# VectorE's order in a fused attention and feed-forward kernel: one maximum ahead of the shares, and the finish of y ahead of the masking

## What is computed

```python
x = x + conv_ref(ln_over_channels(x))       # clustering attention
t = tokens(x)
t = t + ffn_ref(layernorm(t))               # feed-forward, 96 -> 384 -> 96
return images(t)

# conv_ref, for each head and each quarter image (28 x 28 tokens)
centers = pooled(f)                         # 4 x 4 centers
sim = sigmoid(beta + alpha * cosine(centers, tokens))
sim = sim * one_hot(argmax over centers)    # "masked"
agg = (sim @ v + vc) / (sim.sum + 1)        # "reciprocal", "shares"
out = sim.T @ agg, then the projection Wp and its bias

# ffn_ref
h = quantize(norm(t) @ sign(W1) + b1)       # scale: largest |h| of a group of 6 images
y = quantize(gelu(h) @ sign(W2) + b2)       # scale: largest |y| of the group
# quantize(a) = clip(a * 128 / (largest + 1e-5), +-(128 - 1e-5))
```

## Time and profile before

| | us |
|---|---|
| median of 3 runs | 3051.05 |
| lowest and highest | 3048.34, 3052.36 |
| the profiled execution's own time | 3054.72 |
| its span in the trace | 3052.90 |

### The profile page before, as it was taken

The page is one execution under the profiler, slowest core; times in us unless marked ns, Lnnn a source line. Parts: engine busy times, 40 slices in busy tenths (PEclk is TensorE's granted clock), DMA queues, the critical chain, the costliest instruction groups (busy, mean ns, idle before and its releaser), DMA issues.

```text
span 3052.9 us, 62593 instructions
## 1 busy us (share of the span) xinstructions
PE 2839.2 (93%) x20918; PEld 1957.2 (64%) x20918; DVE 2680.4 (88%) x5540; ACT 2172.5 (71%) x4510; POOL 1869.5 (61%) x4275
## 2 busy tenths in 40 slices
PE   3999999999999999999999999999999999999984
PEld 2666676556666765666666666666655766666553
DVE  3788888899999989899998999999989999998954
ACT  2677777887777779767776977677788777677941
POOL 1566666347777753677776357777734777774353
PEclk9999999999999999999999999999999999999976
DMA  1011111002222210222221012222100222220024
GB/s 44 17 38 36 33 33 33 9 17 65 65 65 65 70 44 1 65 69 74 67 64 49 1 49 65 65 64 65 57 25 17 68 74 67 71 66 25 17 72 135
DMA packets 30932, 154.29 MB, mean 51 GB/s; under 512 B 6483, under 2 KB 6804, under 8 KB 30612
## 3 DMA queue, kind: packets, MB, share of 16 engines
q1 hardware_dynamic: 30612, 150.28, 17.8%
HBM read 75.60 MB, written 74.66 MB: 49 GB/s over the span
## 4 chain that ended last, share of the span: by engine, by line
PE 49%; POOL 30%; issue 9%; DVE 9%; ACT 1%; DMA 0%; SPq 0%; POOLq 0%; DVEq 0%
PE ps L948 18%; PE ps L1025 8%; PE ps L1080 8%; POOL mo_x L379 6%; PE ps L901 5%; DVE st_x L658 5%; PE ps L920 4%; POOL mo_x L374 3%; PE ps L1008 3%; DVE cenx L667 3%; POOL n2c L394 2%; PE ps L965 1%; PE ps L931 1%; POOL ninv L425 1%; POOL nxy L417 1%
## 5 line engine op out<-in xcount | busy, mean ns | idle before, releaser
L948 PE MATMUL ps<-wfT,xn 97*112 97x384 f32 x1792 | 730.8, 516 | 0.1
L1025 PE MATMUL ps<-tok,w1T 98*128 98x392 f16 x2880 | 617.1, 338 | 6.4 <-ACT turns L577 1.6
L518 ACT ACTIVATE sq<-ps 112x384 f32<-112x384 f32 x896 | 431.9, 490 | 226.9 <-PE ps L948 224.2
L769 DVE TENSOR_REDUCE hmax<-ps 128x1 f32<-128x392 f32 x720 | 383.6, 561 | 49.2 <-PE ps L1025 28.4
L1025 PEld LDWEIGHTS ps<-tok,w1T 98*128 98x128 f16 x2880 | 275.3, 99 | 229.9 <-issue 76.0
L702 DVE TENSOR_REDUCE n<-sq 112x32 f32<-112x1536 f32 (+1 forms) x256 | 396.3, 1548 | 20.6 <-ACT sq L518 6.6
L948 PEld LDWEIGHTS ps<-wfT,xn 97*112 97x112 f32 x1792 | 284.8, 182 | 180.2 <-issue 55.7
L574 ACT ACTIVATE turns<-ps,scale 128x1176 f32<-128x1176 f32 x240 | 363.5, 1515 | 45.3 <-DVE scale L792 39.8
L463 POOL CAST turns<-turns 128x392 f16<-128x392 f32 x240 | 169.6, 707 | 353.8 <-ACT turns L574 343.8
L524 ACT ACTIVATE sig<-cosb,betac 112x896 f32<-112x896 f32 x128 | 133.4, 1042 | 317.9 <-DVE cosb L712 317.9
L487 ACT ACTIVATE xnT<-ps,mo_x 112x96 f32<-112x96 f32 x896 | 305.2, 455 | 72.5 <-POOL mo_x L381 72.5
(11 more groups left out here) (141 smaller groups left out, 6174.7 us busy)
## 6 DMA issues: line engine op xcount, KB each, us to landing
xbuf<-in_x SPq DMA_DIRECT2D x64, 588.0 KB, 4.8
out<-xbuf SPq DMA_DIRECT2D x64, 588.0 KB, 6.0
turns<-out SPq DMA_DIRECT2D x60, 588.0 KB, 6.4
out<-turns SPq DMA_DIRECT2D x60, 588.0 KB, 4.4
tok<-in_L_ffn_W SPq DMA_DIRECT2D x2, 142.5 KB
cst<-in_constants SPq DMA_DIRECT2D x1, 195.0 KB
wf<-in_L_conv_Wf SPq DMA_DIRECT2D x1, 144.0 KB
tok<-in_L_conv_Wv SPq DMA_DIRECT2D x1, 144.0 KB
```

Source lines behind the costliest of these rows:

```text
L518: nc.scalar.activation(sq[:, t, :], bank(2 + t % 2, TN, D), ACT.Square).then_inc(f_sq, 1)
L769: v.tensor_reduce(o, bank(6 + u % 2, 128, HT), AX.X, ALU.max, apply_absolute_value=True)\
L948: mm(bank(2 + t % 2, TN, D), xn[:, k % 2, t * TN:(t + 1) * TN], wfT[:, :], start=True, stop=True)\
L1025: ins = mm(dst, w1T[:, c * 128:(c + 1) * 128], tok[:, bass.ds(place, 1), part, s * HT:(s + 1) * HT].rearrange("p a n -> p (a n)"), start=p ...
```

## The change

Two lists in other engines are only broken into lines differently. VectorE's list changes in two places: `h_largest(2, 3)` moves from behind `shares` to between `denominators` and `shares`; and `finish(part)` moves from behind `masked` to ahead of it. Nothing else changes; each step does what it did.

```diff
-                         (R, 1, h_largest(0, 2), FFN), (A, 1, denominators), (A, 1, shares),
-                         (R, 1, h_largest(2, 3), FFN), (R, 1, h_largest(3, 5), FFN),
...
-                         (X, 0, stats("x", 0)), (A, 0, masked), (R, 0, finish(part), FINAL)]
+                        (R, 1, h_largest(0, 2), FFN), (A, 1, denominators), (R, 1, h_largest(2, 3), FFN),
+                        (A, 1, shares), (R, 1, h_largest(3, 5), FFN), (X, 1, pooled), (M, 1, cosine),
...
+                        (X, 1, q_placed), (M, 0, norms(0, TA)), (X, 0, stats("x", 0)), (R, 0, finish(part), FINAL),
+                        (A, 0, masked)]
```

More of the change, by code:

```diff
@@ L452, in attention @@
                 return [(X, 1, moments("x", EPS_C)), (M, 1, norm_guess), (M, 1, newton), (M, 1, cubic),
-                         (X, 1, center_squares), (R, 0, clipped(g, part), FINAL), (X, 1, center_norms),
-                        (A, 0, marks), (R, 0, moments("t", EPS_T), FFN)]
+                        (X, 1, center_squares), (R, 0, clipped(g, part), FINAL), (X, 1, center_norms), (A, 0, marks),
+                        (R, 0, moments("t", EPS_T), FFN)]
             def group(g, part):
@@ L556, in attention @@
                         (A, 1, copy_sim(1)), (R, 1, n_high(1, part), FFN), (X, 1, normalise("x", 0, 0)),
-                        (X, 1, normalise("x", 0, 1)), (X, 1, copy_x(0)), (X, 1, copy_x(1)),
-                        (A, 0, sigmoid), (M, 0, squares(0, 2)), (X, 0, gather), (M, 0, squares(2, 5)),
-                        (A, 0, copy_eq), (M, 0, squares(5, 7)), (R, 0, normalise("t", 6, 0), FFN)]
+                        (X, 1, normalise("x", 0, 1)), (X, 1, copy_x(0)), (X, 1, copy_x(1)), (A, 0, sigmoid),
+                        (M, 0, squares(0, 2)), (X, 0, gather), (M, 0, squares(2, 5)), (A, 0, copy_eq),
+                        (M, 0, squares(5, 7)), (R, 0, normalise("t", 6, 0), FFN)]
             act.wait_ge(w_loaded, 16 * LOADS)
@@ L815, in attention @@
                 return [(M, 1, norms(TA, T)), (R, 1, n_low(0), FFN), (R, 1, n_low(1), FFN), (A, 1, summed),
-                         (R, 1, h_largest(0, 2), FFN), (A, 1, denominators), (A, 1, shares),
-                         (R, 1, h_largest(2, 3), FFN), (R, 1, h_largest(3, 5), FFN),
[L818 to L821, removed]
-                         (X, 0, stats("x", 0)), (A, 0, masked), (R, 0, finish(part), FINAL)]
+                        (R, 1, h_largest(0, 2), FFN), (A, 1, denominators), (R, 1, h_largest(2, 3), FFN),
+                        (A, 1, shares), (R, 1, h_largest(3, 5), FFN), (X, 1, pooled), (M, 1, cosine),
+                        (X, 1, centers), (A, 1, residual(0)), (R, 1, h_largest(5, 6), FFN), (A, 1, residual(1)),
+                        (X, 1, center_floor), (A, 0, maxima), (X, 1, q_scaled), (R, 0, stats("t", 6, g), FFN),
+                        (X, 1, q_placed), (M, 0, norms(0, TA)), (X, 0, stats("x", 0)), (R, 0, finish(part), FINAL),
+                        (A, 0, masked)]
             def group(g, part):
```

## The result

The changed kernel takes 3089.95 us (median of 4 runs, 3089.74 to 3091.61); the kernel before, with one more run on the same chip, 3049.73. The ratio is 1.0127, with a 95% interval from 1.0115 to 1.0139: 40 us slower, where the prediction had 50; its range was 3082 to 3121. The profiled execution has a span of 3087.9 us, 35.0 more than before. The 5 us between 35 and 40 lie in the profiled execution of before, which took 3054.72, that is 5.0 above its kernel's median; that of the changed kernel (3089.74) is at its median.

The account below looks back on a forecast made before the run. It took TensorE's written order and its exchanges with VectorE to bound the kernel. Finish +45, third maximum +5 and last part 0 made +50 on the median of 3051.05: 3101 us, range 3082 to 3121.

Parts of the forecast that it names:

- the round between TensorE and VectorE: Steady-state slots of 18.40 us: set by TensorE's written order and its exchanges with VectorE, not by VectorE's amount of work.
- The finish ahead of the masking: VectorE behind st_x: masked starts 0.94 us later, scores cover part, L981 starts 0.47 later, paid again in each slot.
- Paid in 96 slots: +45: Four middle groups of 24 slots, one finish each: 96 x 0.47 = +45 us, from +40 to +51.
- The third maximum: VectorE, between reciprocal and shares: wait for tile 4 swallows all but 0.04 us; 120 slots make +5, from 0 to +12.
- The last part: Slots with three finishes: four lose +5, filled waits and an earlier end gain; net 0, from -5 to +6 us.
- POOL: Beside the finish: L366 is blocked, costing about the 0.63 us that L374 saves, so POOL gains nothing.
- TensorE's idle time ahead of centers: Rival: the 0.45 us idle there swallows the delay, 3053 to 3058 us; chance 0.07 together with an inert swap.
- The clock in the middle slots: Rival: TensorE's granted clock of 1.00 falls there; 2 us a slot would make +190, 3290 us; chance 0.02.
- POOL's case: Rival: POOL's chain sets the slot and L366 runs freely: -60 us, 2991, or 3021 half blocked; chance 0.04.

Follow-up runs that it names:

- The probe behind the masked step: Kernel before plus one unread VectorE maximum over constants (900 elements) behind the masked step in 24 first-group slots: 3041.49 against 3041.69 us, ratio 1.0003.
- the same probe ahead: Kernel before plus the same 900-element maximum between st_x and the masked step in 24 first-group slots: 3052.53 against 3041.69 us, ratio 1.0033.
- short probe: Kernel before plus an unread VectorE maximum of 420 elements ahead of the masked step in first-group slots: 3041.45 against 3041.69 us, ratio 0.9997.
- half a finish: Kernel before with each middle-group finish cut in two, 392 columns ahead of the masked step and 392 behind: 3051.23 against 3041.69 us, ratio 1.0029.

## Why the prediction was right, and where its sizes were off

- **VectorE's amount doesn't set the slot; the round between TensorE and VectorE does.** Right. The probe behind the masked step adds about 1 us of work in each slot for nothing, and the same probe ahead costs 0.50 a slot.
- **The finish ahead of the masking: 0.94 late, 0.47 of it paid.** Right, a little too dear. The masked step moved by 0.93; the middle of 0.42 and 0.53 was taken, and 0.43 was right, the one by the matmuls' start. From the masked step's end to L980's weight loads it is 0.05 us in all the slots that wait; the 0.06 came from rounded starts.
- **Paid in 96 slots: +45.** The slots give 96 x 0.43 = 41. From first to last masked step, the four groups grew by 35.5 and not by 92 x 0.43 = 40, as each group of before had 1.1 us in longer slots at the edges of its loop (19.27, 18.65), most of which the changed kernel lacks. The stretches between groups, which the sum left out, add 5.1 from pair to pair: some 2 for the slots in them, the rest unexplained. Their total varies as much without any change of order in the middle groups, from 657.0 (short probe) to 662.2 us (the maximum's move alone).
- **The third maximum: +5, from 0 to +12.** The mis-sized term: it is 0 (ratio 1.0007, slots unchanged). The working itself found that the wait for tile 4 swallows all but 0.03 to 0.04; that remainder came from taking starts to the hundredth and a spacing of 0.24, where the shares' is 0.22. A remainder of the size of the reading error should have been counted at 0. Had the sum been made of 0.43 and 0, it would have been 3092 with the last part at 0. That this is so near the measured 3090 is partly luck: in the profiles the first group (-1.9) and the last part (-3.7) offset the stretches between groups (+5.1).
- **The last part: 0, from -5 to +6.** In the profiles -3.7 from the first pair on, within the bounds. Its terms: the fifth slot -2.1 (predicted -2.2), the end -3.5 (predicted -1 to -3), and the four slots +1.9 (predicted +5, from 0 to +9), which is 2.83 for the three finishes ahead of the first masked step less 0.9 in the slots behind it. This last term hangs on TensorE's clock, which the prediction held at 0.71: the four slots from masked to masked took 89.5 to 94.2 us in profiles of the new order and 87.0 to 95.1 in those of the old. By the two comparisons of the move in the last part alone it is worth 1.5 to 2.3 us, with intervals that include 1.
- **POOL.** L366 rose to a median of 0.94 us and L374 fell to 0.20, as worked out. The Trainium skill's rule on the port that VectorE and GpSimd share ("SBUF — State Buffer", section "SBUF: two separate sides") held on both: the finish, with two SBUF inputs, blocked L366, and the probe, with one, didn't (0.22). With half a finish (0.60) L366 took 0.53. The probe shows that the late masked step is paid with POOL free as well.
- **The rivals.** TensorE's idle time ahead of centers stayed 0.45 (L919 at 1441.46 and 1460.30 in the changed kernel) and swallowed nothing, as cenx moved with L980. The clock in the middle slots stayed 1.00, with 0.93 us of TensorE idle in each (18.83 less 17.90). No middle slot got shorter, as POOL's case would have had it.

## What to carry to other kernels

Before a step is moved ahead of one that releases another engine, read two times from one slot: when the release comes, and when the other engine would have become free for it. The difference is a cover that can be spent once; beyond it a delay in a loop bound by a round of two engines was paid nearly in full in every slot here. Work of the same length behind the release can be free; in slots that really wait, as in the last two here, the same move gains.

## What the runs showed of the hardware

- TensorE's granted clock in the last part is not a matter of the order alone: the same program showed slots of 26.8, 21.1, 26.8, 19.5 us (granted 0.62, 0.92, 0.62, 0.91) and of 22.0, 25.3, 22.7, 19.6 (0.84, 0.66, 0.77, 0.91). At 1.00 granted, a slot of the old order takes 19.55 us, at 0.71 23.66.
- A stall of 0.25 us in TensorE's matmuls ahead of L980 (0.46 at its weight loads), besides the 0.45 ahead of centers, left the granted clock at 1.00 in the middle groups.
- Where TensorE waits for `sim`, its weight loads start some 0.05 us after the end of VectorE's masked step: in the 101 waits of the changed kernel as in the one wait of the kernel before.
- VectorE's finish, with two SBUF inputs, stretched a small POOL instruction from 0.22 to 0.94 us; a VectorE maximum of about the same length with one SBUF input left it at 0.22.
